# A scan block with a slot table on one core: long jobs in two halves, later reads, another head

## The reference

```python
xn = rmsnorm(x, rms_w); xi, z = split(xn @ in_proj)
xi = silu(causal_conv4(xi) + conv_b)
dt, Bm, Cm = split(xi @ x_proj); delta = softplus(dt @ dt_w + dt_b)
# per step t:  h = exp(delta*A)*h + (delta*xi)*B ;  y = sum_s h*C
y = (y + xi*D) * silu(z); x = x + x_kept + y @ out_proj
x = x + ffn(attention(x, cond, mask))      # one row per batch
```

## Time and profile before

| | |
|---|---|
| median of 3 runs | 588.54 us (585.46 to 591.59) |
| profiled execution | 589.81 us, span 588.0 us, mean granted clock of TensorE 0.931 |
| first scan starts | 50.44 us |
| the four chunks' first scans | 50.4, 172.5, 288.9, 403.8 us |
| last scan ends | about 518.3 us |
| busy: TensorE / VectorE / ScalarE / GpSimd | 82 / 83 / 60 / 60% of the span |

### The profile page before, as it was taken

The page is one execution under the profiler, slowest core; times in us unless marked ns, Lnnn a source line. Parts: engine busy times, 40 slices in busy tenths (PEclk is TensorE's granted clock), DMA queues, the critical chain, the costliest instruction groups (busy, mean ns, idle before and its releaser), DMA issues.

```text
span 588.0 us, 7947 instructions
## 1 busy us (share of the span) xinstructions
PE 482.2 (82%) x2801; PEld 345.7 (59%) x2801; DVE 488.0 (83%) x575; ACT 354.5 (60%) x619; POOL 355.2 (60%) x213
## 2 busy tenths in 40 slices
PE   5877899778758999896689998966896856989992
PEld 5522665455548676564576765546775644978761
DVE  4858999999999989989988899899999989761522
ACT  4476566669775766786756768877466466421210
POOL 5007959956886599678755987778567657000001
PEclk9996999978998999979999998799998889599998
DMA  8202101110011011110110110111101940028004
GB/s 292 94 24 91 70 3 64 44 38 36 37 36 37 1 41 71 36 37 36 38 36 11 59 42 37 36 37 36 37 37 37 348 196 1 2 79 341 1 1 148
DMA packets 17918, 38.87 MB, mean 66 GB/s; under 512 B 1665, under 2 KB 10497, under 8 KB 17874
## 3 DMA queue, kind: packets, MB, share of 16 engines
q1 hardware_dynamic: 17874, 38.32, 18.3%
HBM read 36.08 MB, written 2.23 MB: 65 GB/s over the span
## 4 chain that ended last, share of the span: by engine, by line
PE 38%; DVE 31%; issue 16%; ACT 10%; POOL 2%; DMA 1%; SPq 1%; DVEq 0%; POOLq 0%; ACTq 0%
DVE scanmem L1606 18%; DVE yTd L1622 7%; PE hT L769 7%; PE pp L493 5%; PE pp L515 4%; PE yacc L549 4%; PE pp L575 4%; PE dA L748 3%; POOL scanmem L1279 2%; ACT hc L1158 2%; DMA xt<-in 1%; ACT dA L1148 1%; PE pp L541 1%; PE pp L487 1%; PE pp L719 1%
## 5 line engine op out<-in xcount | busy, mean ns | idle before, releaser
L1279 POOL TENSOR_TENSOR scanmem<-par,scanmem 128x1024 f32<-128x1024 f32 x128 | 299.2, 2363 | 109.3 <-PE hT L769 56.3
L1148 ACT ACTIVATE dA<-par,Aneg 128x512 f32<-128x512 f32 x256 | 172.3, 690 | 69.9 <-DVE scanmem L1606 69.0
L769 PE MATMUL hT<-con,scanmem 128*128 128x128 f32 x1024 | 158.5, 292 | 61.2 <-DVE yTd L1622 39.1
L769 PEld LDWEIGHTS hT<-con,scanmem 128*128 128x128 f32 x1024 | 121.4, 149 | 116.7 <-DVE yTd L1622 52.0
L1606 DVE TENSOR_TENSOR_SCAN scanmem<-dA,carry,scanmem 128x512 f32<-128x512 f32 x128 | 157.0, 1270 | 2.5 <-ACT dA L1148 2.4
L1606 DVE TENSOR_TENSOR_SCAN scanmem<-dA,scanmem 128x512 f32<-128x512 f32 x128 | 149.4, 1210 | 3.7 <-ACT dA L1148 3.3
L1158 ACT ACTIVATE hc<-hT,CTs 128x512 f32<-128x512 f32 x128 | 87.1, 681 | 79.1 <-PE hT L769 78.5
L1622 DVE SCALAR_TENSOR_TENSOR yTd<-hT,CTs,yTd 128x512 f32<-128x512 f32 x120 | 88.1, 734 | 12.0 <-PE hT L769 11.9
L549 PE MATMUL yacc<-con,hc 128*128 128x128 f32 x512 | 79.9, 299 | 6.4 <-ACT hc L1158 6.4
L549 PEld LDWEIGHTS yacc<-con,hc 128*128 128x128 f32 x512 | 65.7, 155 | 10.8 <-ACT hc L1158 7.5
L493 PE MATMUL pp<-xnT,wi 128*128 128x512 f32 x128 | 65.7, 646 | 7.1 <-ACT xnT L945 4.0
(11 more groups left out here) (173 smaller groups left out, 473.1 us busy)
## 6 DMA issues: line engine op xcount, KB each, us to landing
scanmem<-brow SPq DMA_DIRECT2D x32, 512.0 KB, 3.6
par<-in SPq DMA_DIRECT2D x1, 4096.0 KB, 17.6
scanmem<-in SPq DMA_DIRECT2D x1, 4096.0 KB, 14.2
xt<-in SPq DMA_DIRECT2D x4, 512.0 KB, 6.8
wi<-in SPq DMA_DIRECT2D x2, 1024.0 KB, 6.7
out<-par SPq DMA_DIRECT2D x4, 512.0 KB, 4.1
aw<-in SPq DMA_DIRECT2D x5, 256.0 KB, 6.5
xr<-in SPq DMA_DIRECT2D x1, 1024.0 KB, 8.8
```

What stands on the lines that cost most here:

```text
L769: last = nc.tensor.transpose(hT[:, i % 2, m * P:(m + 1) * P], hb[:, n % RING, m, i * P:(i + 1) * P], ident)
L1148: A(dA[:, m % 2, :], delta(c)[:, m, :], ACT.Exp, scale=Aneg[:, m * NS + s:m * NS + s + 1]).then_inc(da_ready, 1)
L1279: nc.gpsimd.tensor_tensor(hb[:, n % RING, ms, :], dx(c)[:, ms, :], Bb[:, row:row + 1, :].to_broadcast([P, 2, T]), ALU.mult).then_inc(bx_re ...
```

## The change

- V, X and O become halves (`IN_TWO`): in the loop TensorE issues the first half at the end of the slot before (`begin`), the second in the job's own slot (`end`).
- VectorE reads V, D and Z (`LATE`) one slot later than before, directly after that slot's two scans and ahead of its sum. ScalarE reads them where it did.
- The slot tables move: T to slot 4, I to 5 to 8, V to 10, 12, 14, X to 18, D to 20 to 23 with one per slot, Z to 24 to 27, the first O from slot 11 to slot 3. Z of chunk 0 goes one per slot instead of two.
- Head: T turns the unscaled rows by transposes as soon as they are in. I uses them, its four results lie in four banks (two of them in `dA`), and VectorE multiplies them by the turned row scale (`scl_0`) while reading them; GpSimd multiplies `xnT` by it before Z. TensorE takes conv tiles 2 and 3, VectorE 0 and 1. The counts 4 to 7 go behind the conv, the squares of batch 1 behind the copy of the scale. D uses four banks and the softplus runs over pairs of tiles. Idle products are 8 of zeros at the very start, then 2, 2 and 3, where there were 18 and 6.
- Tail: the idle products after R, A, W12, WT, H and HT are fewer (`WARM` drops from 39 to 22 of them), and the mask comparison follows the softmax of batch 1 instead of the read of VV.

```diff
-PROLOGUE = {3: [("T", 0), ("T", 1)], 4: [("I", 0)], 5: [("I", 1)], 6: [("I", 2)], 7: [("I", 3)], 8: [("V", 0)],
-            10: [("V", 2)], 12: [("V", 3)], 14: [("X", 0)], 18: [("XT", 0), ("D", 0)], 20: [("D", 1), ("D", 2)], 21: [("D", 3)],
-            22: [("Z", 0)], 23: [("Z", 1)], 24: [("Z", 2)], 25: [("Z", 3)]}
-EPILOGUE = {1: [("Y", 1), ("Y", 3)], 11: [("O", 0)], 16: [("O", 1)], 28: [("R", 0)], 30: [("R", 1)]}
+PROLOGUE = {4: [("T", 0), ("T", 1)], 5: [("I", 0)], 6: [("I", 1)], 7: [("I", 2)], 8: [("I", 3)], 10: [("V", 0)],
+            12: [("V", 2)], 14: [("V", 3)], 18: [("X", 0)], 20: [("XT", 0), ("D", 0)], 21: [("D", 1)], 22: [("D", 2)], 23: [("D", 3)],
+            24: [("Z", 0)], 25: [("Z", 1)], 26: [("Z", 2)], 27: [("Z", 3)]}
+EPILOGUE = {1: [("Y", 1), ("Y", 3)], 3: [("O", 0)], 16: [("O", 1)], 28: [("R", 0)], 30: [("R", 1)]}
 LAST_EPILOGUE = {1: [("Y", 1)], 2: [("Y", 3)], 3: [("O", 0)], 5: [("O", 1)], 17: [("R", 0)], 19: [("R", 1)]}
 ATT = [6, 8, 8, 10, 12, 14, 15, 16, 17, 20, 22, 23, 24, 27]
 ATT1 = [28, 29]
-HEAD_CONV = 3
+HEAD_CONV = 2
+EARLY_I = [2, 3, 0, 1]
 POOL_TILE = 1
 POOL_AT = [4, 5]
...
-    head = [("F", 0, 0)]
-    head += [("T", 0, k) for k in range(KD)] + [("I", 0, m) for m in range(CT)] + [("V", 0, m) for m in range(HEAD_CONV, CT)]
-    head += [("X", 0, 0), ("XT", 0, 0)] + [("D", 0, m) for m in range(CT)]
+    head = [("T", 0, k) for k in range(KD)] + [("F", 0, 0)] + [("I", 0, m) for m in EARLY_I] + [("V", 0, m) for m in range(HEAD_CONV, CT)]
+    head += [("X", 0, 0)] + [("D", 0, m) for m in range(CT)] + [("XT", 0, 0)]
     beside = [[] for _ in range(2 * NCH * NS)]
     for c in range(NCH):
         at = 2 * c * NS
         if c == 0:
             for m in range(CT):
-                beside[m // 2] += [("Z", 0, m)]
-            beside[4] += [("TP", 0, 0)]
-            beside[6] += [("U", 0, 0)]
+                beside[m] += [("Z", 0, m)]
+            beside[3] += [("TP", 0, 0)]
+            beside[5] += [("U", 0, 0)]
...
+IN_TWO = ("V", "X", "O")
+LATE = ("V", "D", "Z")
+
+
 def to_read(h):
 
     return BESIDE[h - 1] if h else []
 
 
+def read_by_vector(h):
+
+    return [job for job in to_read(h) if job[0] not in LATE]
+
+
+def read_late(h):
+
+    return [job for job in to_read(h - 1) if job[0] in LATE] if h else []
+
+
+def begun(h):
+
+    return [job for job in BESIDE[h + 1] if job[0] in IN_TWO] if h + 1 < len(BESIDE) else []
+
+
 
 WARM = {**{(name, 1, 0): 2 for name in ("GT", "M", "RR", "PT", "YV", "YT", "VV", "WO")}, ("G", 1, 1): 2,
-        ("S1", 1, 0): 12, ("R", 3, 0): 4, ("R", 3, 1): 4, ("A", 1, 1): 4, ("W12", 0, 0): 9, ("WT", 0, 0): 6, ("H", 1, 0): 4, ("HT", 1, 0): 2,
-        ("H", 2, 0): 4, ("HT", 2, 0): 2}
-WARM_HEAD = [18, 6]
+        ("S1", 1, 0): 12, ("R", 3, 0): 3, ("R", 3, 1): 4, ("A", 1, 1): 1, ("W12", 0, 0): 3, ("WT", 0, 0): 3, ("H", 1, 0): 3, ("HT", 1, 0): 1,
+        ("H", 2, 0): 3, ("HT", 2, 0): 1}
+WARM_ZEROS = 8
+WARM_HEAD = {"mag": 2, "V": 2, "X": 3}
 
 
...
         def bank(job):
+            name, n, m = job
+            if n == 0 and name == "I" and m >= 2:
+                return dA[:, m - 2, :]
+            if n == 0 and name == "D" and m >= 2:
+                return hT[:, m - 2, :]
             return pp[:, INDEX[job] % 2, :]
 
...
+                if n == 0:
+                    if k == 0:
+                        pe.wait_ge(s_x[0], 16)
+                        pe.wait_ge(s_vec, 32)
+                    for i in range(NT):
+                        last = nc.tensor.transpose(o[:, i * P:(i + 1) * P], xt[:, i, k * P:(k + 1) * P], ident)
+                    return last
...
             def job_Z(job, o):
                 _, n, m = job
+                if n == 0 and m == 0:
+                    pe.wait_ge(xn_scaled, KD)
                 return in_proj(n, o, DI + m * P)
...
+                for k in taps:
                     last = mm(o, dg[:, m, k, :], xr3[:, m, k:k + T], start=k == 0, stop=k == KC - 1)
...
+                    if m < 2:
+                        wait_read(pe, (("T", 0, 1), ("F", 0, 0))[m])
+                elif n == 0 and name == "D" and m >= 2:
+                    pe.wait_ge(mag_act, 2)
+                elif q >= 2:
+
                     pe.wait_ge(job_free[q % 2], q // 2)
 
...
+            def begin(job):
+                wait_free(job)
+                name = job[0]
+                if name == "V":
+                    job_V(job, bank(job), range(0, 2))
+                elif name == "X":
+                    job_X(job, bank(job), range(0, 2))
+                else:
+                    job_O(job, bank(job), range(0, 1))
+
...
+            def beside(h):
+
+                for job in BESIDE[h]:
+                    if job[0] in IN_TWO:
+                        end(job)
+                    else:
+                        run(job)
+                for job in begun(h):
+                    begin(job)
...
+
+            pe.wait_ge(pads_zero, 1)
+            zeros = a_sb[:, :, :].rearrange("p i h -> p (i h)")
+            for _ in range(WARM_ZEROS):
+                mm(hT[:, 1, 0:GB * QR], zeros[:, 0:P], zeros, start=True, stop=True)
+            for k in range(KD):
+                run(("T", 0, k))
+            pe.wait_ge(ss_act, 4)
+            pe.wait_ge(ss_dve, 4)
+            squares_turned(0, yacc)
+            run(("F", 0, 0))
+            keep_warm(WARM_HEAD["mag"], hT[:, 1, 0:P])
+            for m in EARLY_I[0:2]:
+                run(("I", 0, m))
+
+            pe.wait_ge(scl_ready, 1)
+            for i in range(NT):
+                last = nc.tensor.transpose(hT[:, 0, i * P:(i + 1) * P], scl[:, i:i + 1].to_broadcast([P, P]), ident)
+            last.then_inc(scl_turned, 1)
+            for m in EARLY_I[2:]:
+                run(("I", 0, m))
+            for m in range(HEAD_CONV, CT):
+                run(("V", 0, m))
+            keep_warm(WARM_HEAD["V"], hT[:, 1, 0:P])
+            pe.wait_ge(ss_act, 12)
+            pe.wait_ge(scl_row, 1)
+            squares_turned(1, hT)
+            run(("X", 0, 0))
+            keep_warm(WARM_HEAD["X"])
+            for m in range(CT):
+                run(("D", 0, m))
+            run(("XT", 0, 0))
...
+            def first_softplus(pair):
+
+                d = delta(0)[:, 2 * pair:2 * pair + 2, :]
+                if pair == 0:
+                    for m in range(2):
+                        wait_full(act, ("D", 0, m))
+                        own.mark(A(delta(0)[:, m, :], bank(("D", 0, m)), ACT.Abs))
+                else:
+                    wait_full(act, ("D", 0, 3))
+                    own.mark(A(d, hT[:, :, :], ACT.Abs))
+                own.after()
+                own.mark(A(d, d, ACT.Exp, scale=-1.0))
+                own.after()
+                A(d, d, ACT.Ln, bias=1.0).then_inc(head_sp_ready, 1)
...
+            act.wait_ge(scl_turned, 1)
+            A(scl_0, hT[:, 0, :], ACT.Copy).then_inc(scl_row, 1)
             for g in range(GB, 2 * GB):
                 act.wait_ge(ss_act, 4 + g - GB)
                 square(g)
             rstd(1)
+            act.preload_act_table_set("exp_and_others")
+            read(("V", 0, 2))
+            conv_tanh(0, 0)
+            read(("V", 0, 3))
+            conv_tanh(0, 1)
+            exp_ln_table()
+            read(("X", 0, 0))
             act.wait_ge(mag_pe, 2)
             for i in range(2):
                 A(magrow[:, i * 512:(i + 1) * 512], hT[:, i, :], ACT.Copy).then_inc(mag_act, 1)
-            for job in HEAD:
...
+            pool.wait_ge(scl_row, 1)
+            wait_read(pool, ("V", 0, CT - 1))
+            for k in range(KD):
+                nc.gpsimd.tensor_tensor(xnT[:, k, :], xnT[:, k, :], scl_0, ALU.mult).then_inc(xn_scaled, 1)
...
+            def scale_first(m):
+
+                job = ("I", 0, m)
+                wait_full(dve, job)
+                V.tensor_tensor(xr3[:, m, KC - 1:], bank(job), scl_0, ALU.mult).then_inc(freed(job), 1)
...
-                if job == ("VV", 1, 0):
-                    compare_rows()
+                    if job[1] == 1:
+                        compare_rows()
...
+                if g == 1:
+                    read(("F", 0, 0))
...
-            first_scaling()
+            dve.wait_ge(scl_row, 1)
+            for m in EARLY_I:
+                scale_first(m)
+            dve.wait_ge(half_ready, 2)
+            for m in range(HEAD_CONV):
+                conv_taps(0, m, range(KC))
+            conv_finish(0, 0)
+            read(("V", 0, 2))
+            read(("V", 0, 3))
+            conv_finish(0, 1)
...
                     scan_step(n, 1)
+                    for job in read_late(2 * n):
+                        read(job)
                     if n:
                         mac_step(n - 1, 1)
-                    for job in to_read(2 * n):
+                    for job in read_by_vector(2 * n):
                         read(job)
                     scan_step(n, 2)
                     scan_step(n, 3)
+                    for job in read_late(2 * n + 1):
```

(20 more changed lines are left out.)

102 lines of the change are left out of this document (50 added, 52 removed).

## The result

The changed kernel took 603.0 us (median of 4 executions, 600.1 to 605.4), the kernel before 590.1 us beside it: a ratio of 1.023, 95% interval 1.016 to 1.030. The forecast was 576.0. The change makes the kernel slower, where faster was forecast; the interval lies wholly above 1, though not wholly above 1.02.

What follows compares the result with a forecast made beforehand. No single engine bound it: TensorE and VectorE were both busy over four fifths. Gains 5.0 + 2.2 + 2.9 - 0.5 + 3.0 = 12.6 took 589.8 to 577.2, less 1.3: 576 us, range 570 to 581.5.

Steps and rivals of the forecast that it cites:

- After the read they have about a slot (3.5 us) before that sum asks: Late reads: TensorE's next job and transposes, 2.6 us for Z, fit before VectorE's sum at full clock; cost nothing.
- signs of being wrong: First scan not before 47, Z rows over 2.5 us per job in later chunks, or VectorE's idle unchanged in slots 9-18.
- D's stretch: Slots 21 to 25: one D per slot leaves ScalarE 20.1 us of work against 21.6; 1.2 us won in third chunk.
- Stall moves from the read to the scan: D read late: VectorE's scan would wait for an exponential queued behind the softplus, and the 0.6 us read follows.
- 20.0 us against 21.6: Third chunk, slots 12 to 18: with halves in neighbouring slots VectorE is the bound by a hair; 1.6 us won.
- The wait for GpSimd at slot 12: Third chunk: GpSimd's chain behind I's later read ends at 332.7, so savings of slots 9 to 11 become VectorE's wait.
- 0.4 us net: O's tile 0 in slot 3: its first half waits for VectorE's read of Y, taken as 0.4 us net.
- about 2.2 us: Chunk 0: T in slot 4 waits for the bank of Z's tile 3, read in slot 5; about 2.2 us given back.
- Head and tail: Head: first scan at 44.2, 6.2 us earlier. Tail: fewer idle products and an earlier mask comparison, 3.0 us won.
- No wait above 5 us arises, so I keep the full clock: Tail: with fewer idle products TensorE has no wait above 5 us, so its clock stays full; 3.0 us won.
- Slower: late reads with a cold clock: Rival: 1.2 GHz of the D stretch lasts through Z, costing some 17 to 20 us, so 594 us; chance 0.06.
- 1.6 per job: Cold-clock rival: a Z job and its transposes take 5.1 us against a slot's 3.5, losing 1.6 per job.

Runs made afterwards that it cites:

- E1: The changed kernel with only the late reads undone (V, D and Z read in the slot after the job): 581.1 us, 0.988 of the kernel before.
- E11: E5 with V and X whole as well, so no halves at all, on the new slot tables: 576.1 us, 0.978 of the kernel before.
- E4: The changed kernel with only O's first job moved back from slot 3 to slot 11 in chunks 1 and 2: 603.4 us, 1.026.
- E5: E1 with O issued whole and chunk 0's Z two per slot: 576.6 us, 0.978 of the kernel before.
- E7: The changed kernel with only D read late: ten executions from 585.6 to 598.1 us, median 596.1 us.
- E8: The changed kernel with only Z read late: 589.8 us, 1.002 of the kernel before.
- E6: The changed kernel with only V read late: 583.4 us, 0.991 of the kernel before.

## Why the prediction was wrong

**Step that failed: "After the read they have about a slot (3.5 us) before that sum asks; ... I cost it at nothing."** I looked for the next one to ask for the transposes and took VectorE's sum. ScalarE's scaling asks first, and in its queue stand the next exponentials, on which the next scans wait, behind which I had just put the read. The slack was no slot but what is left of the ring. And "at the full clock" did not hold behind the wait. It cost 13.8 us in chunk 0, 6.7 in chunk 1 and 6.2 in chunk 2 (after less E1), 26.7 in all, where the profiled spans miss the forecast by 25.3. Of that, 1.7 each in chunks 1 and 2 lie in slots 3 to 5, where no read is late and TensorE's clock fell in the changed kernel and not in E1; whether earlier late reads bring that fall on is not shown. The rest is this one term, costed at nothing. Without the late reads (E1) slots 6 and 18 of chunk 0 start at 72.5 and 120.8, where 74.0 and 120.5 were forecast; in the changed kernel they start at 79.5 and 127.7. One of the prediction's own signs of being wrong showed too, Z0 of the third chunk at 2.91 us.

**D's stretch, 1.0, 0.8 and 1.2 us won in chunks 0, 1 and 2.** Right in the table part: slots 19 to 30, which hold D and Z in both tables, take 0.8, 2.0 and 0.9 us less in E1 than before, though in chunks 1 and 2 TensorE's clock has a hand in the size. Reading late was no part of the gain, as I had it, but took it away: after the change the same slots take 5.5, 2.4 and 3.1 us more than before. "Stall moves from the read to the scan" was seen, and not followed on.

**Halves.** "20.0 us against 21.6" for slots 12 to 18: measured 19.9. The wait for GpSimd at slot 12 is there, 1.39 us. The cause I gave is wrong: with whole jobs (E11) chunk 2 needs 0.9 us more in slots 9 to 18. What relieved these slots is that O's 3.4 us left them: with O back in 11 (E4) slots 12 to 14 take 14.1 us for 9.9.

**O to slot 3, "0.4 us net".** Mis-sized: slots 3 to 5 took 4.1 us more than before in both chunks (15.1 for 11.0). 1.1 of it is the first half ahead of the transposes (E1 against E5, which in these chunks differ there only in O). 1.7 is the clock (15.1 against E1's 13.4, with the same instructions and no late read): the transposes at 314.07 above took 1.91 us, those of E1 in that place 1.04. The rest, 1.3, is the tables: O comes in, and T and I go a slot later. Slots 9 to 14 give it back.

**Chunk 0, "about 2.2 us" for T behind Z3.** The stall I named is the row at 72.11, and is 4.36 us with the late read and 1.6 without (E1). Before it stands one that I did not see: Z2 waits 5.66 us for Z0's late read. Both then ran at the low clock, 3.78 us each, where E1 has 1.88 and 2.05.

**Head and tail.** First scan 44.0 (forecast 44.2), tail 2.6 us shorter (forecast 3.0). The counts begin at 9.21 (forecast 9.3). In the changed kernel the tail kept the full clock for as long as TensorE had work (to 590.3 us; the clock fell at 592.9), as said. In E1 it fell at 526.1 us for 10.2 us, and there the tail took 74.3 us, 4.7 more. "No wait above 5 us arises, so I keep the full clock" doesn't tell the two apart: TensorE's longest wait behind the last scan is 0.8 us in both, and no run shows that 5 us is a bound. The windows of E1, 20 us behind the last scan's start:

```profile
524.70:529.70 5.00, 4.91 (x31) 4.34 (x30) 0.42 (x1) 0.42 (x2) 0.00 (x0) 0.64 1.03 402
529.70:534.70 5.00, 5.00 (x20) 4.39 (x21) 0.19 (x1) 0.28 (x1) 0.00 (x0) 0.50 0.33 116
```

The same place in the changed kernel:

```profile
551.10:556.10 5.00, 4.91 (x44) 4.19 (x43) 0.61 (x2) 0.42 (x2) 0.00 (x0) 1.00 1.04 393
556.10:561.10 5.00, 5.00 (x22) 3.01 (x23) 1.99 (x3) 0.28 (x1) 0.00 (x0) 1.00 0.13 47
```

**The rivals.** "Slower: late reads with a cold clock" was nearest, at a chance of 0.06. Its size was 17 to 20 us, and the late reads cost 22; its time of 594 is still 9 short of 603.0. Its "1.6 per job" is seen in D, 1.8 us more for a D and its transposes at half the clock. I made it hang on the clock alone and on Z, and judged the clock likely to hold. But the wait needs no cold clock to start: D1 and its transposes ran at the full clock, and then D2 stood for 3.92 us. With the clock low in both, slots 22 to 24 are still 2.7 us longer with late reads. I have no run that parts the two for the whole 22 us.

## What to carry to other kernels

Before moving a read behind other work of its engine, list who waits for the buffer that it frees, and follow that queue until it comes back to the engine: if it does, the work put ahead of the read is in a ring with it, and the ring's length can become the slot. Here, with two alternating banks and one job per slot, a read behind the scans of two slots on was too late for D and Z (E7, E8), and with a job in every second slot it hardly mattered (V, E6). Where a forecast says that a wait "has a slot", check it against the first asker of each engine, not against the one in view. And a remedy that adds work, as idle products do, can hide what it gives: compare the same slots at two clocks where the traces have both.
